# Layer 0 of a two-layer perceiver kernel: from rows of whole tiles to one list of half tiles on the same three rotating PSUM banks

## The chip, the cores and the metric

One core of one Trainium2 chip. The metric is the device time of the whole kernel in microseconds (us). Engines: PE (TensorE, matmuls, with PEld for its weight loads), DVE (VectorE), ACT (ScalarE), POOL (GpSimd), SP (SyncE, issues the DMAs).

## The reference, cut to what matters

A block of two layers over a latent x [128, 256] and a context of 12544 rows of 192. The change touches the first cross attention alone:

```python
def _L0_xattn_ref(query, key_value, Wq, bq, Wk, bk, Wv, bv, Wo, bo):   # 16 heads of 16
    q = (query @ Wq + bq).reshape(B, Nq, H, D).transpose(0, 2, 1, 3)
    k = (key_value @ Wk + bk).reshape(B, Nkv, H, D).transpose(0, 2, 1, 3)
    v = (key_value @ Wv + bv).reshape(B, Nkv, H, D).transpose(0, 2, 1, 3)
    attn = jnp.einsum('bhqd,bhkd->bhqk', q, k) * scale
    attn = jnp.clip(attn, -CLAMP, CLAMP)
    attn = jax.nn.softmax(attn, axis=-1)
    x = jnp.einsum('bhqk,bhkd->bqhd', attn, v).reshape(B, Nq, Cq)
    return x @ Wo + bo
```

Behind it come a gated attention, a feed-forward with ternary weights, and the same three for layer 1.

## The kernel before

**Tiling of layer 0.** The 12544 context rows are worked in 14 chunks (NCH) of 896 columns (CH), each of 7 tiles (TPC) of 128 keys, each tile in two halves (HALVES = 14 per chunk) of 8 heads. All 128 queries and 16 heads are done at once, with a running maximum per head, so a chunk needs its maxima before its scores. A round of the loop therefore scores and weighs chunk c and prepares chunk c + 1. The letters of the work, as the kernel's list names it:
- K (4 per chunk, `project0`): a key block, 5 matmuls of 448 columns; ACT writes its high part (`key_block_hi`), DVE its low part (`key_block_lo`). SP then stacks the keys by 12 DMAs (`stack_keys`).
- m (32, `unit_scores`): one matmul over 32 rows that gives a head's (and its pair's) scores of half a chunk; DVE takes the maximum (`unit_max`, L918). Four neighbours lie in four row groups. Behind m 18 and m 31 DVE merges the maxima (`half_maxima`, L926 to L936).
- V (7, `values0`): a tile of values, 5 matmuls of 256; ACT copies it (`value_tile`).
- R (4, `minus_max_row`): minus the maxima as rows, cast by ACT into the queries' extra row (`max_row`). The diagonal that R multiplies is made by POOL for the first half (`spread_half`, L469) and by DVE for the second.
- L: whether any maximum is so large that clipping is needed (`large_sum`, `clip_flag`). With these inputs it is not, and `clip_half` is branched over.
- F (`factors`): how far the maximum fell, transposed; ACT copies it, DVE rescales the running sum in bank 4 (`rescale`, L995).
- S (14 halves, `scores0`): 4 matmuls of 256 into banks 0 and 1 or 2 and 3; ACT takes the exponential of 1024 columns (`exponentials`, L668).
- W (14 halves, `weigh0`): 8 float32 products (16 records) of 17 weight columns, added up in bank 4.

ACT also casts the raw context of chunk c + 2 to its high part (`split_hi0`, L607 and L609), POOL then makes the low parts (`split_lo0`, L457 and L460), and SP loads the next raw chunk.

**What sets the order.** Every engine has its own in-order queue, written out from one list, `LIST`: one row for each of the 7 tiles. K, F, m, V, R and L take the three PSUM banks 5 to 7 in turn; `bank_free` makes PE wait for whoever reads the bank's last use. An S in a row is a whole tile (both halves), a W too:

```python
LIST = [["K0", "F", "K1", "S", "K2", "K3", "W", "m", "m", "m", "V0", "V1", "m", "m", "V2", "V3", "m", "m"]]
LIST += [["S", "m", "m", "m", "W", "m", "m"]] * 5
LIST += [["W", "R0", "R1", "V4", "V5", "V6", "R2", "R3", "L", "", "", "S"]]
```

ACT casts both parts of the raw chunk together, behind the first row. POOL's loop makes the spread of chunk c + 1 and then the low parts of chunk c + 2. In the last round nothing is prepared; there PE adds two sums for the feed-forward's ternary thresholds behind the second tile (L1497, L1499), after DVE's two sums over the weights (L1026). From them POOL makes the ternary weights (L508 to L512), while layer 0 ends and the gated attention runs.

Of the kernel before, what the change touches and what calls it, by code (L numbers as in the profile page):

```python
# [22 lines left out]
ALU = mybir.AluOpType  # L23
ACT = mybir.ActivationFunctionType
# [60 lines left out]
def steps():  # L85

    out, n, m = [], 0, 0
    for items in LIST:
        row = []
        for item in items:  # L90
            if item in ("S", "W"):
                row.append((item, 0, None))
                continue
            kind, i = item[:1], int(item[1:] or 0)
            if kind == "m":
                i, m = m, m + 1
            if kind:
                row.append((kind, i, n))
            n += 1
        out.append(row)  # L100
    return out, n


STEPS, USES = steps()
BANKS = 3
USED_BY = {n: (kind, i) for row in STEPS for kind, i, n in row if n is not None}
assert USES % BANKS == 0


def use_bank(n):  # L110
    return 5 + n % BANKS


def bank_of(kind, i):
    return use_bank(next(n for n, use in USED_BY.items() if use == (kind, i)))


def user_before(n):

    at = n - BANKS  # L120
    while at % USES not in USED_BY:
        at -= BANKS
    kind, i = USED_BY[at % USES]
    return kind, i, at < 0
# [29 lines left out]
def perceiver(nc, a, out):  # L154
    with ExitStack() as ctx:
# [273 lines left out]
        def _(pool):  # L429
# [49 lines left out]

            pool.wait_ge(S["qs_rows"], 192)  # L480
            spread_half(0, 0)
            pool.wait_ge(S["e0_dm_half"], 1)
            split_lo0(1, 1)
            pool.wait_ge(S["e0_lo"], 3)
# [95 lines left out]
        def _(act):  # L580
# [21 lines left out]
            def split_hi0(c, b, half=None):  # L602

                if half != 1:
                    act.wait_ge(S["e0_raw"], 48 * (c + 1))
                    act.wait_ge(S["e0_vproj"], TPC * (c - 1))
                    nc.scalar.copy(ct[:, b, X_AH, :], raw[:, 0, :])  # L607
                if half != 0:
                    nc.scalar.copy(ct[:, b, X_B, :], raw[:, 1, :]).then_inc(S["e0_hi"], 1)  # L609
# [32 lines left out]
            act.wait_ge(S["e0_raw"], 48)  # L642
            nc.scalar.copy(ct[:, 0, X_AH, :], raw[:, 0, :])
            nc.scalar.copy(ct[:, 0, X_B, :], raw[:, 1, :]).then_inc(S["e0_hi"], 1)
            for i in range(4):
                key_block_hi(0, i)
            act.wait_ge(S["v_ones"], 2)
            for t in range(4):
                value_tile(0, 0, t)
            act.wait_ge(S["e0_raw"], 96)  # L650
            nc.scalar.copy(ct[:, 1, X_AH, :], raw[:, 0, :])
            nc.scalar.copy(ct[:, 1, X_B, :], raw[:, 1, :]).then_inc(S["e0_hi"], 1)
            for i in range(2):
                max_row(0, i)
            for t in range(4, TPC):
                value_tile(0, 0, t)
            for i in range(2, 4):
                max_row(0, i)
            fall_spread(0)

            def exponentials(c, b, t):

                for u in (2 * t, 2 * t + 1):
                    g = HALVES * c + u
                    act.wait_ge(S["e0_ok"], g + 1)
                    act.wait_ge(S["e0_score"], g + 29)
                    act.wait_ge(S["e0_pv"], g + 11)
                    nc.scalar.activation(pr[:, (HALVES * b + u) % 4, :], bank(2 * (u % 2), 2), ACT.Exp  # L668
                                         ).then_inc(S["e0_exp"], 1)

            exponentials(0, 0, 0)

            def chunk0(c, b, i2, nxt=True, split=True):

                for t in range(TPC):
                    for kind, i, n in STEPS[t]:
                        if kind == "S" and t < TPC - 1:
                            exponentials(c, b, t + 1)
                        elif kind == "F":
                            factor_copy(c)  # L680
                        elif not nxt:
                            continue
                        elif kind == "S":
                            fall_spread(c + 1)
                            exponentials(c + 1, 1 - b, 0)
                        elif kind == "K":
                            if i == 0:
                                act.wait_ge(S[f"e0_keys{b}"], 192 * (i2 + 1))
                                act.wait_ge(S["e0_head"], UNITS * (c + 1))
                            key_block_hi(c + 1, i)  # L690
                        elif kind == "V":
                            if i == 0:
                                act.wait_ge(S["e0_pv"], HALVES * (c + 1))
                            value_tile(c + 1, 1 - b, i)
                        elif kind == "R":
                            if i % 2 == 0:
                                act.wait_ge(S["e0_score"], HALVES * (c + 1) + 27 + i // 2)
                                act.wait_ge(S["e0_row_out"], 16 * (c + 1))
                            max_row(c + 1, i)
                    if split and t == 0:  # L700
                        split_hi0(c + 2, b)

# [3 lines left out]
            chunk0(NCH - 2, 0, NSUP - 1, split=False)  # L706
            chunk0(NCH - 1, 1, NSUP - 1, nxt=False, split=False)
# [115 lines left out]
        def _(dve):  # L823
# [88 lines left out]
            def unit_max(c, m, n):  # L912

                h, half = unit_of(m)[4], unit_of(m)[3]
                if m % 16 == 0:
                    dve.wait_ge(S["e0_chain"], 8 * c)
                dve.wait_ge(S["e0_head"], UNITS * c + m + 1)
                V.tensor_reduce(cu2[:, h, half:half + 1], ps[:, use_bank(n), 0:NB], AX_X, ALU.max  # L918
                                ).then_inc(S["e0_red"], 1)
# [44 lines left out]
            def prepare(c, b, t, flag):  # L964

                for kind, i, n in STEPS[t]:
                    if kind == "S" and (t < TPC - 1 or c < NCH):
                        clip(c - 1 + (t + 1) // TPC, (t + 1) % TPC, flag)
                    elif c == NCH:
                        if kind == "K" and i == 1:  # L970
                            rescale(c - 1)
                    elif kind == "K":
                        key_block_lo(c, i)
                        if i == 1 and c > 0:
                            rescale(c - 1)
                    elif kind == "m":
                        unit_max(c, i, n)
                        if i == 18:
                            half_maxima(c, b, 0)
                        if i == UNITS - 1:  # L980
                            half_maxima(c, b, 1)
                            after_maxima(c, b)
                    elif kind == "L":
                        flag = clip_flag(c)
                        with dve.If(flag < 1):
                            dve.sem_inc(S["e0_ok"], HALVES)
                            dve.sem_inc(S["clip_min"], HALVES)
                            dve.sem_inc(S["clip_max"], HALVES)
                return flag

# [21 lines left out]
            def clip(c, t, flag):  # L1012

                if flag is not None:
                    with dve.If(flag > 0):
                        clip_half(c, 2 * t)
                        clip_half(c, 2 * t + 1)

            flag = None
            for c in range(-1, NCH):  # L1020
                for t in range(TPC):
                    flag = prepare(c + 1, (c + 1) % 2, t, flag)
                    if c == NCH - 1 and t == 0:
# [270 lines left out]
        def _(pe):  # L1294
# [37 lines left out]
            def bank_free(c, n):  # L1332

                kind, i, earlier = user_before(n)
                x = c - 1 if earlier else c
                if kind == "K":
                    pe.wait_ge(S["e0_klo"], 4 * x + i + 1)
                elif kind == "F":
                    pe.wait_ge(S["e0_factor_sb"], c)
# [6 lines left out]
                elif kind == "L":  # L1346
                    pe.wait_ge(S["e0_clipf"], x + 1)
# [458 lines left out]
```

## Time and profile before

| | |
|---|---|
| median of 3 runs | 920.91 us (920.09 to 921.3) |
| the profiled execution | 919.66 us, span 917.8 us |
| granted TensorE clock, mean | 0.97 |
| PE busy | 857.3 us (93%) |
| DVE busy | 628.9 us (69%) |
| ACT busy | 427.2 us (47%) |
| POOL busy | 217.6 us (24%) |

The span runs from the first to the last instruction of the profiled execution. Busy times are unions of an engine's instructions; matmuls overlap each other, so the distance between their starts tells more than their durations. The second tenth of the span to its middle (some 60 to 515 us) is the rounds of layer 0.

### The profile page before, as it was taken

The page shows a single profiled execution, that of the slowest core. Times are in us where ns is not written, and L with a number is a line of the kernel's source. Part 1 is how long each engine was busy: PE and PEld are TensorE (multiplying, and loading weights), DVE is VectorE, ACT ScalarE, POOL GpSimd, SP SyncE. Part 2 cuts the span into 40 slices and gives each one's busy share as a digit, 9 for nine tenths or more (in the row PEclk, how much of TensorE's full clock was granted, in tenths as well). Part 3 has the DMA queues.
Part 4 walks back from the last instruction along what each step waited for, and adds up shares of the span by engine and source line. Part 5 has one row for each costly group of instructions (what it writes and reads, how often), then busy time and mean ns, then how long its engine had stood idle before and what let it go on. Part 6 is the DMA issues. An engine that isn't in the chain of part 4 may idle for free.

```text
span 917.8 us, 21933 instructions
## 1 busy us (share of the span) xinstructions
PE 857.3 (93%) x7662; PEld 663.3 (72%) x7662; DVE 628.9 (69%) x1104; ACT 427.2 (47%) x578; POOL 217.6 (24%) x233
## 2 busy tenths in 40 slices
PE   3889999999999999999999988998999999999798
PEld 2567777777777777777777757654688887888676
DVE  5768568568568568567567643699487878777373
ACT  2245765765765766766765721300233333333122
POOL 4182022022022022022020392350033232222000
PEclk9669999999999999999999999999999999999798
DMA  5845645645645645648635133210000000000000
GB/s 178 197 128 124 180 114 120 178 115 120 175 118 120 172 120 120 170 123 211 168 85 122 48 139 106 81 39 1 7 19 13 18 14 19 13 19 7 1 1 7
DMA packets 43867, 85.16 MB, mean 93 GB/s; under 512 B 11616, under 2 KB 26657, under 8 KB 41889
## 3 DMA queue, kind: packets, MB, share of 16 engines
q1 hardware_dynamic: 43822, 84.62, 35.9%
q8 instruction: 21, 0.34, 0.2%
q14 instruction: 24, 0.19, 0.1%
HBM read 45.03 MB, written 0.25 MB: 49 GB/s over the span
## 4 chain that ended last, share of the span: by engine, by line
PE 69%; issue 12%; DVE 10%; POOL 4%; ACT 2%; SPq 1%; DMA 1%; DVEq 0%; ACTq 0%; POOLq 0%
PE ps L1642 9%; PE ps L1455 9%; PE ps L1467 8%; PE ps L1373 8%; PE ps L1363 7%; PE ps L1356 6%; DVE cu L918 6%; PE ps L1650 5%; PE ps L1663 5%; PE ps L1643 2%; PE ps L1382 1%; PE ps L1389 1%; POOL ffw L510 1%; POOL wraw L508 1%; PE ps L1616 1%
## 5 line engine op out<-in xcount | busy, mean ns | idle before, releaser
L918 DVE TENSOR_REDUCE cu<-ps 128x1 f32<-128x448 f32 x448 | 250.4, 618 | 53.2 <-PE ps L1373 51.2
L668 ACT ACTIVATE pr<-ps 128x1024 f32<-128x1024 f32 x196 | 190.1, 1023 | 66.4 <-PE ps L1455 65.6
L435 POOL TENSOR_TENSOR pause<-pause 128x1 f32<-128x1 f32 x41 | 12.8, 314 | 569.5 <-DVE mr L930 377.5
L1373 PE MATMUL ps<-khl,qp 32*128 32x448 f32 x448 | 123.9, 483 | 2.6 <-DVE khl L908 0.8
L1455 PE MATMUL ps<-qs,ks 128*128 128x256 f32 x784 | 122.6, 296 | 3.3 <-ACT qs L627 3.1
L1455 PEld LDWEIGHTS ps<-qs,ks 128*128 128x128 f32 x784 | 101.9, 190 | 21.7 <-issue 20.6
L1467 PE MATMUL ps<-pr,v 128*17 128x128 f32 x3136 | 104.6, 274 | 0.5 <-DVE ps L995 0.5
L1642 PE MATMUL ps<-ks,ct 128*128 128x512 f32 x352 | 98.2, 400 | 0.3 <-ACT pr L788 0.3
L1467 PEld LDWEIGHTS ps<-pr,v 128*17 128x17 f32 x3136 | 77.2, 97 | 22.2 <-issue 19.1
L1373 PEld LDWEIGHTS ps<-khl,qp 32*128 32x128 f32 x448 | 57.9, 188 | 48.9 <-DVE cu L918 14.0
L908 DVE SCALAR_TENSOR_TENSOR khl<-ps,bk,khl 128x448 fp32r<-128x448 f32 x56 | 37.1, 682 | 74.5 <-ACT khl L615 74.5
L1206 DVE TENSOR_SCALAR ps<-ps 128x1024 f32<-128x1024 f32 x44 | 54.1, 1229 | 46.2 <-PE ps L1643 46.2
L788 ACT ACTIVATE pr<-ps 128x1024 f32<-128x1024 f32 x44 | 45.3, 1030 | 81.3 <-DVE ps L1206 81.3
L1642 PEld LDWEIGHTS ps<-ks,ct 128*128 128x128 f32 x352 | 64.8, 189 | 17.6 <-issue 3.4
L1363 PE MATMUL ps<-wv,ct 128*128 128x256 f32 x490 | 72.9, 298 | 4.5 <-DVE cu L918 3.6
L1363 PEld LDWEIGHTS ps<-wv,ct 128*128 128x128 f32 x490 | 65.3, 194 | 15.3 <-DVE cu L918 7.9
L1356 PE MATMUL ps<-ct,wk 128*128 128x448 f32 x280 | 68.9, 387 | 2.1 <-DVE khl L908 2.1
L621 ACT COPY v<-ps 128x256 f32<-128x256 f32 x98 | 36.6, 374 | 60.3 <-PE ps L1363 59.1
L1189 DVE TENSOR_TENSOR pr<-pr,wraw 128x1024 f32<-128x1024 f32 x45 | 55.0, 1223 | 4.0 <-issue 4.0
L1356 PEld LDWEIGHTS ps<-ct,wk 128*128 128x128 f32 x280 | 52.5, 198 | 6.4 <-DVE khl L908 2.5
L1193 DVE TENSOR_TENSOR nm<-nm,pr 128x1024 f32<-128x1024 f32 x45 | 55.4, 1232 | 1.5
L1173 DVE CUSTOM_DVE_ANT_0 pr<-ps,khl 128x1024 f32<-128x1024 f32 x48 | 55.5, 1220 | 0.0
(263 smaller groups left out, 1143.7 us busy)
## 6 DMA issues: line engine op xcount, KB each, us to landing
ks<-khl SPq DMA_DIRECT2D x168, 224.0 KB, 4.9
nm<-maxima SPq DMA_DIRECT2D x14, 1024.0 KB, 4.6
raw<-in_ctxT SPq DMA_DIRECT2D x14, 448.0 KB, 3.9
raw<-in_ctxT SPq DMA_DIRECT2D x28, 224.0 KB, 4.4
ffw<-in_mask_q SPq DMA_DIRECT2D x1, 1568.0 KB, 9.6
raw<-in_ctxT SPq DMA_DIRECT2D x12, 128.0 KB, 2.2
raw<-in_ctxT SPq DMA_DIRECT2D x22, 64.0 KB, 1.8
raw<-in_ctxT SPq DMA_DIRECT2D x44, 32.0 KB, 2.0
```

What stands on the lines that cost most here:

```text
L668: nc.scalar.activation(pr[:, (HALVES * b + u) % 4, :], bank(2 * (u % 2), 2), ACT.Exp).then_inc(S["e0_exp"], 1)
L918: V.tensor_reduce(cu2[:, h, half:half + 1], ps[:, use_bank(n), 0:NB], AX_X, ALU.max).then_inc(S["e0_red"], 1)
L1173: nc.vector.tensor_tensor_reduce(out=junk[:, h % 2], in0=ps[:, 2 * (h % 4):2 * (h % 4) + 2, :], in1=negm[:, b, :].bitcast(F32).rearrange(" ...
L1189: V.tensor_tensor(sl, sl, mk[:, u // 2, :].unsqueeze(1).to_broadcast([P, 8, T]), ALU.mult).then_inc(S["e1_masked"], 1)
L1193: V.tensor_tensor(acc, acc, pr[:, u, :], ALU.add).then_inc(S["e1_sum"], 1)
L1206: V.tensor_scalar(bank(2 * (u % 2), 2), bank(2 * (u % 2), 2), 80.0, None, ALU.min).then_inc(S["e1_ok"], 1)
L1356: last = mm(dst, wk0[:, w, t * P:(t + 1) * P], ct[:, b, xx, half * NB:(half + 1) * NB], start=(j == 0), stop=(j == 4))
L1363: last = mm(ps[:, use_bank(n), 0:C], ct[:, b, xx, t * P:(t + 1) * P], wv0[:, w, :], start=(j == 0), stop=(j == 4))
L1373: mm(ps[:, use_bank(n), 0:NB], qp[part, t, e, :], khl[part, 0, t, half * NB:(half + 1) * NB], start=True, stop=True).then_inc(S["e0_head"], 1)
L1455: last = mm(ps[:, 2 * z + k // 2, (k % 2) * 256:(k % 2) * 256 + 256], ks_v[:, b, gg, t * P:(t + 1) * P], qs[:, gg * 256:gg * 256 + 256], s ...
L1467: last = mm(ps[32 * j:32 * j + 17, 4, (h // 4) * T:(h // 4 + 1) * T], v17_v[:, b, t, h, :], pr[:, (HALVES * b + u) % 4, k * T:(k + 1) * T] ...
L1642: mm(ps[:, 2 * z + j, :], cu[:, t, xx, :], asp[:, w, cols], start=(i == 0), stop=False)
```

## The change

The list becomes one sequence of words, cyclic over rounds, with S and W as single halves; every other word means what it did (X is DVE's rescale, H one of ACT's two casts of the raw chunk, E ACT's exponential of the fall of the maxima, _ a bank left out). The K of the next chunk still stand in front, now with V0 ahead of them and V1 behind. The head and the tail of layer 0 are the same list with what has no chunk left out, instead of code of their own. Banks 0 to 3 are booked by the same table as banks 5 to 7. On POOL the low parts of chunk c + 2 come before the spread of chunk c + 1. ACT's two casts stand apart. The two sums for the thresholds stand behind W7 of the last round, DVE's sums over the weights behind S3.

```diff
-LIST = [["K0", "F", "K1", "S", "K2", "K3", "W", "m", "m", "m", "V0", "V1", "m", "m", "V2", "V3", "m", "m"]]
-LIST += [["S", "m", "m", "m", "W", "m", "m"]] * 5
-LIST += [["W", "R0", "R1", "V4", "V5", "V6", "R2", "R3", "L", "", "", "S"]]
+ORDER = (
+    "V K K F S X K K V W m m m S V H m m S m m W W m m m S S W m m m W S V m m W W _ m m H m S W m m "
+    "S S m m W S m m S m V m m m R W R m m W m m V S V _ W W R R L W E S S "
+).split()
...
             with pool.Fori(2, NCH, 2) as c:
                 for b in range(2):
+                    split_lo0(c + b, b)
+                    pool.wait_ge(S["e0_lo"], c + b + 2)
                     spread_half(c + b - 1, 1 - b)
-                    split_lo0(c + b, b)
...
+                    elif kind == "H":
+                        split_hi0(x, xb, i)
+                    elif kind == "K":
+                        if i % 2 == 0 and (not isinstance(c, int) or x > 0):
+                            act.wait_ge(S[f"e0_keys{1 - xb}"], 192 * (x2 + xb))
+                            act.wait_ge(S["e0_head"], UNITS * (x - 1) + 8 * i + 16)
+                        key_block_hi(x, i)
...
+                    if isinstance(c, int) and c == NCH - 1 and (kind, i) == ("W", 7):
+                        pe.wait_ge(S["e0_red"], UNITS * NCH)
...
-                if t == 1:
-                    pe.wait_ge(S["e0_red"], UNITS * NCH)
```

PE's queue in the middle of a round (S is L1455, m L1373, W L1467; REGISTER_ALU are PE's waits with a computed count). Before:

```order
L1455 MATMUL ps<-qs,ks 128x256 x4
L1452 REGISTER_ALU
L1455 MATMUL ps<-qs,ks 128x256 x4
L1343 REGISTER_ALU
L1373 MATMUL ps<-khl,qp 128x448
L1341 REGISTER_ALU
L1373 MATMUL ps<-khl,qp 128x448
L1341 REGISTER_ALU
L1373 MATMUL ps<-khl,qp 128x448
L1463 REGISTER_ALU
L1467 MATMUL ps<-pr,v 17x128 x16
```

After (S is L1402, m L1373, V L1363), behind the first three m of a round:

```order
L1402 MATMUL ps<-qs,ks 128x256 x4
L1339 ISA
L1363 MATMUL ps<-wv,ct 128x256 x5
L1339 REGISTER_ALU
L1373 MATMUL ps<-khl,qp 128x448
L1339 REGISTER_ALU
L1373 MATMUL ps<-khl,qp 128x448
L1332 REGISTER_ALU
L1402 MATMUL ps<-qs,ks 128x256 x4
L1341 REGISTER_ALU
L1373 MATMUL ps<-khl,qp 128x448
```

Where a whole tile of S stood between m and W, a half tile now stands with a V, or alone.

POOL's queue in the loop, one round: the spread is L469, the low parts are L457 and L460. Before:

```order
L466 ISA
L467 REGISTER_ALU [waits e0_chain]
L435 TENSOR_TENSOR pause<-pause 128x1 [waits e0_row]
L469 TENSOR_TENSOR dm<-con,mr 128x1024
L455 REGISTER_ALU
L457 TENSOR_TENSOR ct<-raw,ct 128x896 [waits e0_lo,e0_hi]
L460 TENSOR_TENSOR ct<-raw,ct 64x896 [waits e0_alo]
```

After, the low parts are L479 and L482, the spread is L491:

```order
L479 TENSOR_TENSOR ct<-raw,ct 128x896 [waits e0_lo,e0_hi]
L482 TENSOR_TENSOR ct<-raw,ct 64x896 [waits e0_alo]
L520 REGISTER_ALU
L488 ISA [waits e0_lo]
L489 REGISTER_ALU [waits e0_chain]
L457 TENSOR_TENSOR pause<-pause 128x1 [waits e0_row]
L491 TENSOR_TENSOR dm<-con,mr 128x1024
```

The low parts no longer wait behind the maxima (e0_chain), and the spread waits behind both.

PE's queue in the last round, up to the two sums (F is L1389, the sums are L1497 and L1499). Before:

```order
L1389 MATMUL ps<-con,wraw 128x128 x4
L1455 MATMUL ps<-qs,ks 128x256 x8
L1467 MATMUL ps<-pr,v 17x128 x16
L1455 MATMUL ps<-qs,ks 128x256 x8
L1467 MATMUL ps<-pr,v 17x128 x16
L1497 MATMUL ps<-con,cnt 49x1
L1499 MATMUL ps<-wsum,con 128x2
```

After (the sums are L1461 and L1463):

```order
L1402 MATMUL ps<-qs,ks 128x256 x4
L1414 MATMUL ps<-pr,v 17x128 x8
L1402 MATMUL ps<-qs,ks 128x256 x8
L1414 MATMUL ps<-pr,v 17x128 x16
L1402 MATMUL ps<-qs,ks 128x256 x8
L1414 MATMUL ps<-pr,v 17x128 x16
L1402 MATMUL ps<-qs,ks 128x256 x4
L1414 MATMUL ps<-pr,v 17x128 x16
L1402 MATMUL ps<-qs,ks 128x256 x4
L1414 MATMUL ps<-pr,v 17x128 x8
L1461 MATMUL ps<-con,cnt 49x1
L1463 MATMUL ps<-wsum,con 128x2
```

Eight halves of W now stand ahead of the sums, where four stood.

## Rows read from the trace of the kernel before

**Rows 1.** The page: span, and busy time of each engine with its share.

```profile
span 917.8 us, 21933 instructions
PE 857.3 (93%) x7662; PEld 663.3 (72%) x7662; DVE 628.9 (69%) x1104; ACT 427.2 (47%) x578; POOL 217.6 (24%) x233
```

**Rows 2.** One line's instructions: the rescale; count, durations in ns, first and last start.

```profile
L995 DVE TENSOR_TENSOR ps<-ps,wraw x14: 689/690/699, 66.6 to 513.5; 128x512 f32<-128x512 f32 x14
```

**Rows 3.** Ten rounds: length, busy us by engine, granted clock, DMA share, GB/s.

```profile
132.30:477.68 345.38, 338.69 (x3811) 263.57 (x3810) 236.59 (x480) 232.00 (x331) 62.03 (x40) 1.00 0.56 141
```

**Rows 4.** The timeline of PE, one round: start, us, what, idle before it.

```profile
198.79 0.73 PE L1455 MATMUL ps<-qs,ks 128*128 128x256 f32 x4
199.74 0.73 PE L1455 MATMUL ps<-qs,ks 128*128 128x256 f32 x4 [0.21 <-ACT qs L627]
...
203.36 1.12 PE L1455 MATMUL ps<-qs,ks 128*128 128x256 f32 x8
204.31 2.19 PE L1356 MATMUL ps<-ct,wk 128*128 128x448 f32 x10
206.43 1.07 PE L1467 MATMUL ps<-pr,v 128*17 128x128 f32 x32
207.43 0.98 PE L1373 MATMUL ps<-khl,qp 32*128 32x448 f32 x3
208.68 1.46 PE L1363 MATMUL ps<-wv,ct 128*128 128x256 f32 x10 [0.27 <-DVE cu L918]
...
215.14 0.62 PE L1373 MATMUL ps<-khl,qp 32*128 32x448 f32 x2
215.69 1.22 PE L1455 MATMUL ps<-qs,ks 128*128 128x256 f32 x8
216.84 0.51 PE L1373 MATMUL ps<-khl,qp 32*128 32x448 f32 x3
217.28 1.07 PE L1467 MATMUL ps<-pr,v 128*17 128x128 f32 x32
```

**Rows 5.** The timeline of DVE and POOL around the first half's maxima.

```profile
221.67 0.16 DVE L926 TENSOR_TENSOR cm<-cu 128x8 f32<-128x8 f32 x1
...
222.14 3.40 DVE L918 TENSOR_REDUCE cu<-ps 128x1 f32<-128x448 f32 x6
...
224.40 2.10 POOL L457 TENSOR_TENSOR ct<-raw,ct 128x896 fp32r<-128x896 f32 x1
...
226.58 2.10 POOL L460 TENSOR_TENSOR ct<-raw,ct 64x896 fp32r<-64x896 f32 x1
```

**Rows 6.** L926 over the kernel, and the timeline of DVE and POOL before the first round.

```profile
L926 DVE TENSOR_TENSOR cm<-cu x28: 156/162/3283, 43.4 to 506.4; 128x8 f32<-128x8 f32 x28
...
50.88 3.28 DVE L926 TENSOR_TENSOR cm<-cu 128x8 f32<-128x8 f32 x1
...
50.60 3.53 POOL L489 TENSOR_TENSOR ffw<-ffw 128x1568 int32<-128x1568 int32 x1
```

**Rows 7.** The timeline of the last round, around the two sums.

```profile
514.12 4.47 DVE L1026 TENSOR_REDUCE wsum<-ffw 128x1 f32<-128x2048 f32 x2
514.26 0.79 PEld L1467 LDWEIGHTS ps<-pr,v 128*17 128x17 f32 x32 [0.67 <-DVE ps L995]
...
515.26 1.22 PE L1455 MATMUL ps<-qs,ks 128*128 128x256 f32 x8
...
516.41 1.07 PE L1467 MATMUL ps<-pr,v 128*17 128x128 f32 x32
...
518.64 0.38 PE L1499 MATMUL ps<-wsum,con 128*128 128x2 f32 x2 [0.98 <-DVE wsum L1026]
...
520.06 2.92 POOL L508 TENSOR_SCALAR wraw<-ffw,thr 128x1024 f32<-128x1024 f32 x1 [19.43 <-issue]
```

**Rows 8.** The chain of work that ended last, where it leaves POOL: start, us, what.

```profile
553.77 0.57 POOL rstd L443
554.37 0.42 DVE xn L856
```

More of the change, by code:

```diff
@@ new lines, with order @@
+EARLY_KEYS, EARLY_UNITS = 0, 0
+UNITS = 2 * H
+def order():
+    out, seen, uses = [], dict.fromkeys("SWKVRmHFXEL", 0), 0
+    for word in ORDER:
+        kind = "m" if word[0] == "u" else word[0]
+        ring = 5 + uses % 3
+        uses += word[0] in "mKVRFL_"
+        if kind == "_":
+            continue
+        n = seen[kind]
+        seen[kind] = n + 1
+        if kind == "S":
+            later, i = divmod(n + 2, HALVES)
+            banks = (2 * (i % 2), 2 * (i % 2) + 1)
+        elif kind == "W":
+            later, i, banks = 0, n, ()
+        elif kind == "K":
+            later, i = divmod(n + EARLY_KEYS, 4)
+            later, banks = later + 1, (ring,)
+        elif kind == "m":
+            later, i = divmod(n + EARLY_UNITS, UNITS)
+            later, banks = later + 1, (int(word[1]),) if word[0] == "u" else (ring,)
+        elif kind in "FX":
+            later, i, banks = int(seen["W"] > 0), 0, (ring,) if kind == "F" else ()
+        elif kind == "H":
+            later, i, banks = 2, n, ()
+        else:
+            later, i, banks = 1, n, () if kind == "E" else (ring,)
+        out.append((kind, i, banks, later))
+    assert uses % 3 == 0
+    return out
@@ new lines, with done_in, user_before @@
+STEPS = order()
+USERS = {b: [at for at, step in enumerate(STEPS) if b in step[2]] for b in (0, 1, 2, 3, 5, 6, 7)}
+def done_in(c):
+    return [(at, kind, i, banks, later) for at, (kind, i, banks, later) in enumerate(STEPS)
+            if not isinstance(c, int) or 0 <= c + later < NCH]
+def user_before(c, at, b):
+    users, back = USERS[b], 0
+    k = users.index(at)
+    while not isinstance(c, int) or c - back >= -2:
+        k -= 1
+        if k < 0:
+            k, back = len(users) - 1, back + 1
+        kind, i, _, later = STEPS[users[k]]
+        if not isinstance(c, int) or 0 <= c - back + later < NCH:
+            return kind, i, later - back
+    return None
@@ L127, in unit_of @@
+def bank_of(kind, i):
+    return next(banks[0] for k, n, banks, _ in STEPS if (k, n) == (kind, i))
 def unit_of(m):
@@ L651, in _ @@
[L651 to L701, printed above, removed]
@@ L1407, in weigh_tile @@
-            def weigh_tile(c, b, t):
-                if t == 0:
-                    pe.wait_ge(S["e0_scaled"], c + 1)
-                for z in range(2):
-                    weigh0(c, b, 2 * t + z)
-            def step0(c, b, count, t, first=False, only=None):
-                x, xb = c + 1, 1 - b
-                for kind, i, n in STEPS[t]:
-                    if kind == "S" and not first:
-                        if t < TPC - 1:
-                            tile(c, b, count, t + 1)
-                        elif only is None:
-                            tile(c + 1, 1 - b, count + b, 0)
-                    elif kind == "W" and not first:
-                        weigh_tile(c, b, t)
-                    elif kind not in "SW":
-                        prepare(x, xb, kind, i, n, first, only)
@@ L1428, in prepare @@
[L1428 to L1448 removed]
+                mm(ps[:, n, 0:1], ones, large[:, :], start=True, stop=True).then_inc(S["e0_flag"], 1)
```

284 lines of the change are left out of this document (137 added, 147 removed).

## The prediction

> **What bounds the kernel now.** I read the page first [rows 1]: TensorE (PE) is busy for 93% of a span of 917.8 us, VectorE (DVE) 69%. The change touches layer 0 alone, which is 14 rounds, one per chunk of keys. The line that rescales the running sum once per round starts first at 66.6 and last at 513.5 us [rows 2]: 13 rounds in 446.9 us, 34.4 us each. Inside them [rows 3] PE is busy for 338.69 of 345.38 us at a granted clock of 1.00, DVE for 236.59, ACT for 232.00. So a round is PE's own queue, and only what PE's queue costs or waits for counts.
>
> What PE's 34.4 us consist of is read in the order of its runs [rows 4]. I call K, V, S, R, F, L full forms (128 rows, 128 columns of weights), m the head maxima (32 rows of weights) and W the weighing (17 columns). Starts, not durations, are the measure, since matmuls overlap:
> - Eight matmuls of S between two K take 204.31 - 203.36 = 0.95 us. Eight between two m runs take 216.84 - 215.69 = 1.15. **A stretch of full forms that has m or W on both sides costs 0.20 more.**
> - A run of three m, in three different row groups, takes 217.28 - 216.84 = 0.44. One of two takes 215.69 - 215.14 = 0.55, longer, because the second waited for a bank. So an m run costs 0.44 however short it is, if its banks are free.
> - W for a whole tile takes 207.43 - 206.43 = 1.00.
> - Waits: m x3 and what follows up to V take 208.68 - 207.43 = 1.25 instead of 0.44 (0.8 lost to the low key halves and a bank); the second S half at a round's start comes 199.74 - 198.79 = 0.95 behind the first, where four matmuls after an m or L need some 0.58 (0.4 lost to the cast of the last maxima row).
>
> **The change, in one round.** The same matmuls are issued; what changes is how often PE changes form. Counted in the two lists (cyclically, with F at the start):
> - Stretches of full forms: 8 before, 14 after. 6 x 0.20 = +1.2 us.
> - Stretches of W: 7 before (a whole tile each), 11 after (eight of them half tiles alone). No half alone is in the trace. Between 0 (a half is just half of 1.00) and 0.2 (the price of both ends of a full stretch); I take 0.1, one end. 4 x 0.1 = +0.4.
> - m runs: 13 before, 14 after. +0.4.
> Together **+2.0 us per round**, certain in sign as long as PE is the bound.
>
> Against it stand the waits that go. S0 and S1 of the next chunk now come behind L and a W half, so the cast of the last maxima row has 0.55 us more: -0.4. V no longer stands directly behind the first three m, only the low key halves are waited for: -0.4. In the five regular rounds of S m m m W m m a second or third m waits some 0.1 to 0.25 each (0.55 against 0.44 above); in the new order the m groups are spread as unevenly (2, 2, 3, 3, 2, 3, 2, 2, 2, 2, 1, 3, 2, 2) and three banks are still all there are, while a reduction takes 3.40 / 6 = 0.57 us [rows 5]; I give half of these back, -0.4, and -0.2 for what stood at V and R late in the round. Bounds: nothing (DVE paces m as before) to -3 (every wait goes). I take **-1.4**.
>
> Then the cost that the change brings on POOL. Before, POOL makes the spread (L469) and after it the two low halves of the chunk after next (L457, L460: 224.40 to 228.68) [rows 5], and the three small DVE instructions of the first half of the maxima (from L926, 221.67) come while POOL is idle: 0.16 us for the first. Now POOL does the low halves first, as soon as ACT has cast the second half. ACT's second cast stands behind V3, ahead of m 17; the maxima stand behind m 18. A cast, a signal and two times 2.1 us of POOL cover the next 4 to 5 us, and m 18's reduction is some 3 us behind the cast. So L926 should fall into the second of POOL's instructions. What happens then is in the trace once [rows 6]: L926 began at 50.88 beside POOL's L489 (50.60 to 54.13) and took 3.28 us, until POOL's instruction ended. The reductions from PSUM are not held this way: the six of L918 from 222.14 to 225.54, at 0.57 each, run on beside L457. DVE stands up to 2.1 us, 1.6 by the positions; PE has three banks and some S and W to do in the meantime, which cover about a third: **+1.0** per round, bounds 0 and 2.1. The Trainium skill (GPSIMD Engine Reference, the table of the engine's properties) says that GpSimd shares its SBUF interfaces with VectorE and contends with DVE instructions in a two-port mode or with two SBUF inputs; L926 is one with two SBUF inputs, and the 3.28 us agree.
>
> Sum of a round: 2.0 - 1.4 + 1.0 = +1.6 us, 13 rounds: **+20.8**. I shade it to +1.4 and **+18**, since the list of waits is the softest term and can only be larger than I found.
>
> **The last round.** Its end is not what counts. The thresholds of the FFN weights are made from L1499's sums, and from them POOL works without a pause from 520.06 [rows 7] to 554.34, where the chain of work goes on at DVE's L856 [rows 8]. L1499 stands behind the second W tile and waits for L1026 (514.12 to 518.59): 518.64. Now it stands behind W7. From W0 (514.26, one start before the S x8 at 515.26) PE has S3 S4, W1 W2, S5 S6, W3 W4, S7, W5 W6, S8, W7. S x8 between W takes 516.41 - 515.26 = 1.15, a W tile 1.00, half tiles 0.67 and 0.55: 0.55 + 1.15 + 1.0 + 1.15 + 1.0 + 0.67 + 1.0 + 0.67 + 0.5 = 7.7. So the sums come at about 522.0 on the old scale, with L1026 long done, against 518.64: **+3.3** (bounds +2, if S and W halves cost nothing extra, and +5, if the exponentials hold W7). The tiles behind W7 are hidden under POOL's 34 us as before.
>
> **The start.** The first V is projected while DVE is still held, but ACT copies it ahead of the first two key blocks, which costs about 1 us; in return the V blocks no longer come two at a time between the m there. POOL's low halves ahead of the spread can hold L926 here too. I take **0**, bounds -3 and +3.
>
> Sum: 18 + 3.3 + 0 = +21. The profiled execution took 919.66 us (span 917.8 and 1.9 around it), 1.2 below the median of 920.91; 919.66 + 21 = 941, and on the scale of the median **942 us**.
>
> **Rivals.**
> 1. *No collision with POOL.* If ACT's second cast runs late (V3 late) or early, POOL's instructions miss L926. Then +0.6 per round, 13 x 0.6 + 3.3 = +11: 932. For it: in the old trace L926 took 162 ns in the median of 28 [rows 6]. Against: the places in the lists. Chance 0.22.
> 2. *The waits were the larger part, and the new order is faster.* Where 3 of the about 3.4 us of waits per round go and the changes of form come at half price, the round has 1.0 - 3.0 = -2.0 at best; with a third of a us of collision about -0.8, 13 times: -10, + 3: 914. It decides once more than 2.2 us of waits go in a round. For it: PE's busy share of 98% hides waits, as the 1.25 for three m shows. Against: the 0.20 of the row of S. The Trainium skill (TensorE: Matmul & The Clock Gate, Part 2) says that LDWEIGHTS is pulled ahead of running matmuls when row groups don't conflict or the background buffer is the target; by that rule changes of form between such tiles would be free. The rows of S do not bear it out. Chance 0.17.
> 3. *Nothing to see.* Changes and waits cancel and the collision is small: 919 to 923. Chance 0.06.
> The forecast, forms plus collision, has 0.55.
>
> **How the numbers follow.** Forecast alone: 934 to 953 (+0.9 to +2.2 per round, the last with the collision at full price). With rival 1 below and part of rival 2 the range is 917 to 953. A difference under 0.2% (1.8 us) can't be told from no change. Faster: 0.17; within: 0.05; slower: 0.78.
>
> **What the profile would show.** Right: the rescale line's starts 35.5 to 36 us apart; S x4 between m or W at 0.67 or so; L926's mean far over 0.2 us, beside POOL's low halves; POOL's thresholds starting 3 us later behind the last rescale. Wrong: rounds under 34.4 us, which would mean that my waits were counted too low; L926 at 0.16, which takes out 1.0 per round; or a new wait at R for POOL's spread, which now comes behind 4.2 us of other work and would add to the time.

## The result, and the profile after

The changed kernel takes **982.33 us** in the median of 4 runs (980.82 to 984.26), the kernel before 920.58 beside it (920.09 to 921.3): a ratio of 1.067 [1.066, 1.069] (in brackets, here and below, the 95% interval). The direction is the one predicted. The size is three times it, 62 us where 21 were forecast.

The page of the changed kernel, span and busy times, and the row of the granted clock in 40 slices (they answer to [rows 1]):

```profile
span 981.3 us, 22063 instructions
PE 913.7 (93%) x7662; PEld 683.6 (70%) x7662; DVE 653.5 (67%) x1104; ACT 430.5 (44%) x578; POOL 217.4 (22%) x233
PEclk9669979889898897897997998999999999999898
```

PE has the same 7662 matmuls and is busy for 56 us more. The same work took longer, and the clock's row is full of sevens and eights. The rescale line (it answers to [rows 2]), and the stretch from its first to its last start in both kernels, the windows view with its columns as in [rows 3]:

```profile
L971 DVE TENSOR_TENSOR ps<-ps,wraw x14: 699/700/700, 71.7 to 576.1; 128x512 f32<-128x512 f32 x14
71.70:576.10 504.40, 494.51 (x4938) 361.48 (x4936) 330.04 (x623) 302.27 (x425) 76.90 (x50) 0.90 0.49 121
```

```profile
66.60:513.50 446.90, 437.86 (x4941) 340.22 (x4940) 306.53 (x624) 298.42 (x426) 76.49 (x50) 1.00 0.55 137
```

The span grew by 63.5 us. The first rescale comes 5.1 us later, the 13 rounds take 504.4 instead of 446.9 (**57.5 more**), and what lies behind the last rescale grew from 404.3 to 405.2 (0.9). In the rounds the mean granted clock went from 1.00 to 0.90. PE's idle time in them hardly changed, 446.90 - 437.86 = 9.0 us before and 504.40 - 494.51 = 9.9 after. How one round looks, from 211.3 to 300.0 (2.3 rounds):

```profile
211.30:221.50 10.20, 10.02 (x72) 6.36 (x75) 6.00 (x14) 3.26 (x6) 0.00 (x0) 0.50 0.06 18
221.50:252.20 30.70, 30.13 (x321) 22.64 (x313) 20.11 (x35) 20.65 (x28) 6.24 (x4) 1.00 0.62 154
252.20:259.00 6.80, 6.56 (x46) 3.95 (x47) 3.93 (x10) 1.49 (x3) 0.00 (x0) 0.50 0.00 0
259.00:289.80 30.80, 30.33 (x336) 23.38 (x334) 21.13 (x39) 21.58 (x30) 6.24 (x4) 1.00 0.59 147
289.80:300.00 10.20, 10.02 (x72) 6.36 (x75) 6.00 (x14) 3.27 (x7) 0.00 (x0) 0.50 0.07 20
```

**Once per round TensorE runs at 1.2 GHz** (0.50) instead of 2.4, for 6.8 and 10.2 us in turn, 12 times between the first and the last rescale; in the kernel before the clock between the two is 1.00. What stands ahead of the fall at 252.20: DVE, POOL and PE from 243 (timeline as in [rows 4]).

```profile
245.78 1.63 DVE L929 TENSOR_TENSOR cm<-cu 128x8 f32<-128x8 f32 x1
...
247.72 3.40 DVE L921 TENSOR_REDUCE cu<-ps 128x1 f32<-128x448 f32 x6
...
243.10 2.10 POOL L479 TENSOR_TENSOR ct<-raw,ct 128x896 fp32r<-128x896 f32 x1 [33.00 <-ACT ct L633]
245.28 2.10 POOL L482 TENSOR_TENSOR ct<-raw,ct 64x896 fp32r<-64x896 f32 x1
...
246.28 0.47 PE L1373 MATMUL ps<-khl,qp 32*128 32x448 f32 x2
246.68 0.63 PE L1414 MATMUL ps<-pr,v 128*17 128x128 f32 x16
247.24 0.73 PE L1402 MATMUL ps<-qs,ks 128*128 128x256 f32 x4
248.40 1.00 PE L1373 MATMUL ps<-khl,qp 32*128 32x448 f32 x2 [0.42 <-DVE cu L921]
249.32 0.74 PE L1402 MATMUL ps<-qs,ks 128*128 128x256 f32 x4
249.99 0.47 PE L1373 MATMUL ps<-khl,qp 32*128 32x448 f32 x1
...
252.44 0.79 PE L1382 MATMUL ps<-dm,nsel 128*128 128x512 f32 x1 [0.26 <-DVE cu L921]
253.16 1.06 PE L1414 MATMUL ps<-pr,v 128*17 128x128 f32 x16
```

The collision is where the prediction put it. L929 (L926 of before) begins at 245.78, in POOL's second low half (245.28 to 247.38), and ends with it: 1.63 us instead of the 0.16 of [rows 5]. The next six reductions come late, PE waits 0.42 us for a bank up to 248.40, and 3.8 us behind that the clock falls. S x4 at 247.24 and the m run at 248.40 hold PE for 1.16 and 0.92 us, where the S x4 at 249.32 and the m run at 246.28 hold it 0.67 and 0.40: 1.0 us for the collision. The W half at 253.16 then holds PE until 254.14, 0.98 us; at 246.68 it was 0.56.

### The profile page after: what moved, and what is told of

Read it like the earlier page. It is cut to its first block, busy times and chain, and to the rows that moved or that the text cites. A ratio compares the mean times of both kernels' runs of the same rounds, so it can differ in the third digit from the quotient of the medians.

```text
span 981.3 us, 22063 instructions
## 1 busy us (share of the span) xinstructions
PE 913.7 (93%) x7662; PEld 683.6 (70%) x7662; DVE 653.5 (67%) x1104; ACT 430.5 (44%) x578; POOL 217.4 (22%) x233
## 4 chain that ended last, share of the span: by engine, by line
PE 71%; issue 13%; DVE 10%; POOL 3%; SPq 1%; ACT 1%; DMA 1%; DVEq 0%; POOLq 0%; ACTq 0%
PE ps L1373 10%; PE ps L1414 10%; PE ps L1402 9%; PE ps L1614 9%; PE ps L1363 7%; PE ps L1354 6%; PE ps L1622 5%; PE ps L1635 4%; DVE cu L921 4%; PE ps L1382 3%; PE ps L1615 2%; DVE cm L929 2%; PE ps L1389 1%; POOL wraw L531 1%; POOL ffw L533 1%
## 5 line engine op out<-in xcount | busy, mean ns | idle before, releaser
L672 ACT ACTIVATE pr<-ps 128x1024 f32<-128x1024 f32 x196 | 196.2, 1024 | 105.7 <-PE ps L1402 100.9
L1373 PE MATMUL ps<-khl,qp 32*128 32x448 f32 x448 | 138.6, 518 | 9.5 <-DVE cu L921 7.6
L1402 PE MATMUL ps<-qs,ks 128*128 128x256 f32 x784 | 137.5, 308 | 0.3 <-ACT pr L672 0.2
L1414 PE MATMUL ps<-pr,v 128*17 128x128 f32 x3136 | 127.4, 295 | 1.6 <-DVE ps L971 1.4
L1402 PEld LDWEIGHTS ps<-qs,ks 128*128 128x128 f32 x784 | 108.3, 199 | 26.9 <-issue 20.6
L479 POOL TENSOR_TENSOR ct<-raw,ct 128x896 fp32r<-128x896 f32 x14 | 29.5, 2110 | 405.4 <-ACT ct L633 378.8
L1373 PEld LDWEIGHTS ps<-khl,qp 32*128 32x128 f32 x448 | 60.2, 201 | 67.5 <-DVE cu L921 26.1
L1363 PE MATMUL ps<-wv,ct 128*128 128x256 f32 x490 | 90.8, 324 | 0.1
L1363 PEld LDWEIGHTS ps<-wv,ct 128*128 128x128 f32 x490 | 77.6, 222 | 9.9 <-DVE cu L921 6.4
L791 ACT ACTIVATE pr<-ps 128x1024 f32<-128x1024 f32 x44 | 45.3, 1029 | 81.3 <-DVE ps L1195 81.3
L1354 PE MATMUL ps<-ct,wk 128*128 128x448 f32 x280 | 63.9, 376 | 2.8 <-DVE khl L911 2.8
L457 POOL TENSOR_TENSOR pause<-pause 128x1 f32<-128x1 f32 x41 | 13.5, 331 | 235.1 <-DMA raw<-in_ctxT 161.4
L651 ACT CAST qs<-ps 32x512 fp32r<-32x512 f32 x56 | 31.0, 577 | 58.4 <-PE ps L1382 58.4
## 6 DMA issues: line engine op xcount, KB each, us to landing
ffw<-in_mask_q SPq DMA_DIRECT2D x1, 1568.0 KB, 10.2
```

The lines of the kernel that those rows point to most:

```text
L791: nc.scalar.activation(pr[:, u, :], bank(2 * (u % 2), 2), ACT.Exp).then_inc(S["e1_exp"], 1)
L1354: last = mm(dst, wk0[:, w, t * P:(t + 1) * P], ct[:, b, xx, half * NB:(half + 1) * NB], start=(j == 0), stop=(j == 4))
L1363: last = mm(ps[:, n, 0:C], ct[:, b, xx, t * P:(t + 1) * P], wv0[:, w, :], start=(j == 0), stop=(j == 4))
L1373: mm(ps[:, n, 0:NB], qp[part, t, e, :], khl[part, 0, t, half * NB:(half + 1) * NB], start=True, stop=True).then_inc(S["e0_head"], 1)
L1402: last = mm(ps[:, 2 * z + k // 2, (k % 2) * 256:(k % 2) * 256 + 256], ks_v[:, b, gg, t * P:(t + 1) * P], qs[:, gg * 256:gg * 256 + 256], s ...
L1414: last = mm(ps[32 * j:32 * j + 17, 4, (h // 4) * T:(h // 4 + 1) * T], v17_v[:, b, t, h, :], pr[:, (HALVES * b + u) % 4, k * T:(k + 1) * T] ...
```

## The experiments

All ran beside the kernel before, which took 918.06 to 918.39 us beside e1 to e9; times are medians, ratios are to those. A difference under 2% is called neither faster nor slower here: e3 and e6 to e9 count as the same as before, and e2 is at that border. Their table, with the stretch from the first to the last rescale of one profiled execution each:

| kernel | us | ratio | first rescale | 13 rounds | clock there |
|---|---|---|---|---|---|
| before | 920.58 | | 66.6 | 446.9 | 1.00 |
| after | 982.33 | 1.067 [1.066, 1.069] | 71.7 | 504.4 | 0.90 |
| e1: POOL's loop order undone | 942.51 | 1.026 [1.020, 1.031] | 73.3 | 459.7 | 0.99 |
| e2: ahead of the loop as well | 936.09 | 1.018 [1.014, 1.022] | 68.0 | 464.3 | 0.98 |
| e3: before, POOL's order alone | 918.01 | 1.001 [0.997, 1.004] | 67.6 | 446.9 | 1.00 |
| e4: after, with eight more matmuls | 958.39 | 1.042 [1.037, 1.046] | 73.9 | 476.1 | 1.00 |
| e5: before, with the collision | 962.97 | 1.049 [1.045, 1.053] | 68.0 | 487.9 | 0.95 |
| e6: after's code, old list | 915.76 | 0.997 [0.994, 1.000] | 62.6 | 445.6 | 1.00 |
| e6b: e6 with POOL's old order | 922.04 | 1.004 [1.002, 1.007] | 68.1 | 445.6 | 1.00 |
| e7: a list of my own | 920.29 | 1.003 [1.000, 1.006] | 65.9 | 443.7 | 1.00 |
| e8: a second one | 918.72 | 1.001 [0.998, 1.004] | 72.8 | 440.1 | 1.00 |
| e9: e8 with POOL's new start | 911.51 | 0.994 [0.991, 0.997] | 61.5 | 440.1 | 1.00 |

The 13 rounds are the firm part: e3 and the kernel before have 446.9 both, e6 and e6b 445.6, e8 and e9 440.1. The start and the end are not. The changed kernel, e1 and e4 have the same code up to the first rescale and reach it at 71.7, 73.3 and 73.9 us; e3 has the same code as before behind the last rescale and takes 401.9 us there instead of 404.3. So a difference of 2 us in the start or the end of single profiles tells nothing.

### The list without the collision: e1 and e2

e1 takes POOL's order in the loop back to that of before, and leaves the list:

```
-                    split_lo0(c + b, b)
-                    pool.wait_ge(S["e0_lo"], c + b + 2)
                     spread_half(c + b - 1, 1 - b)
+                    split_lo0(c + b, b)
```

e2 does the same ahead of the loop, where the split of chunk 1 goes back behind the spread.

> The changed kernel with one thing undone: in the loop POOL makes the spread of the maxima before the low parts, as before the change. Theory A (the blocked maxima and the clock that falls behind them): L929 is back at 0.17 us, the stall of PE behind m 21 goes, the granted clock stays at 1.00 in the rounds, a round is 35.0 to 35.6 us instead of 39.3, in all 930 to 940. Rival (the changes of form and short runs themselves make PE too sparse, the clock falls anyway): L929 at 0.17, but the clock still falls once a round, 38 us a round, 965 to 972.

> As the run with POOL's loop order undone, and the same order undone ahead of the loop too (the spread of chunk 0 before the low parts of chunk 1). The first rescale came at 71.7 us after the change and 66.6 before. Theory: POOL's order is the cause there too (L933 stood 6.1 us once), so this run has the first rescale at 66 to 68 and is 4 us under the other. Rival: the V ahead of the keys and the copy of V0 ahead of the key blocks are: the first rescale stays at 70 to 72 and the two runs are equal.

The maxima's line is back at 0.16 us in the rounds, and 40 and 46 us are gone. e1's rounds are as its first theory has them, its time 2.5 us above 940. All rounds but the last and those with a fall take 35.2 to 35.5 us, against 34.5 to 34.7 before. e2's last three have a fall of 6.8 us each, and one of e1's; such a round takes 37.6 to 37.8 (the last of e2 35.6, where the changed kernel's last takes 33.2). The stretch of e2 around one fall:

```profile
434.00:444.00 10.00, 9.67 (x105) 6.46 (x103) 8.07 (x17) 6.85 (x9) 4.99 (x4) 0.99 1.00 295
443.90:450.70 6.80, 6.80 (x48) 4.18 (x49) 3.89 (x10) 1.53 (x3) 1.29 (x1) 0.50 0.49 138
```

and around e1's:

```profile
111.00:131.00 20.00, 19.90 (x229) 13.69 (x227) 15.76 (x30) 13.12 (x17) 4.62 (x4) 1.00 0.67 140
131.00:138.00 7.00, 6.85 (x48) 4.23 (x49) 4.21 (x11) 1.53 (x3) 1.57 (x1) 0.52 0.46 133
```

So two prices: **the list alone costs 0.8 us per round at full clock, a fall of 6.8 us costs 2.3 to 2.4.** This list runs close to a fall even without the collision. **The falls of e1 and e2 need no wait of PE**: ahead of e1's PE is busy for 19.90 of 20 us. They begin beside the first R of the round, where the 6.8-us falls of the changed kernel begin too. What tips the list in three rounds and not in ten isn't seen in these rows.

### POOL's order in the old list: e3 and e5

e3 gives the kernel before POOL's new order in the loop and puts ACT's second cast behind t = 1; e5 puts it behind t = 2. e5's edit:

```
-                    spread_half(c + b - 1, 1 - b)
                     split_lo0(c + b, b)
+                    pool.wait_ge(S["e0_lo"], c + b + 2)
+                    spread_half(c + b - 1, 1 - b)
...
-                    if split and t == 0:
-                        split_hi0(c + 2, b)
+                    if split and t in (0, 2):
+                        split_hi0(c + 2, b, t // 2)
```

> The kernel before, its list untouched, with the collision alone: POOL makes the low parts ahead of the spread in the loop, and ACT's second cast stands one tile later, so that POOL's second low part covers L926. Theory A: L926 at 1.0 to 2.1 us in the rounds, PE stalls behind m 21; if the stall alone brings the clock down, 3 to 5 us a round, 960 to 985. Rival (the clock needs the sparse order of half tiles as well): 0.8 to 1.5 us a round, clock at 1.00, 930 to 940.

> The earlier attempt to bring the collision into the old list missed: POOL was done 1.3 us before L926, which stayed at 0.16 us. Here ACT's second cast stands one more tile later (behind the third), so POOL's second low part should lie over the first half's maxima. List untouched. Theory A (a stall of PE behind blocked maxima brings the clock down by itself): L926 (here L927) at 1 to 2 us, clock at half for 6 to 10 us in each round, 37 to 39 us a round, 950 to 980. Rival (it takes the sparse order of half tiles too): 35.2 to 36 us a round, clock at 1.00, 927 to 940.

e3 missed its aim: POOL's second instruction ended at 221.35, the maxima began at 222.62 and took 0.16 us. It shows only that POOL's order by itself costs nothing in the old list. e5 hit, with 2.03 us for the maxima in 12 rounds, and is 45 us slower than before with the old list and the same matmuls. DVE, POOL and PE of one round:

```profile
236.66 2.03 DVE L927 TENSOR_TENSOR cm<-cu 128x8 f32<-128x8 f32 x1
...
236.57 2.10 POOL L460 TENSOR_TENSOR ct<-raw,ct 64x896 fp32r<-64x896 f32 x1
...
237.19 1.22 PE L1456 MATMUL ps<-qs,ks 128*128 128x256 f32 x8
239.68 1.52 PE L1374 MATMUL ps<-khl,qp 32*128 32x448 f32 x3 [1.27 <-DVE cu L919]
...
242.56 2.08 PE L1456 MATMUL ps<-qs,ks 128*128 128x256 f32 x8
244.56 0.74 PE L1374 MATMUL ps<-khl,qp 32*128 32x448 f32 x3
```

and its clock in the windows view:

```profile
239.00:242.40 3.40, 2.59 (x37) 1.52 (x37) 3.28 (x7) 0.99 (x2) 2.04 (x2) 1.00 0.73 213
242.40:245.80 3.40, 3.40 (x25) 2.55 (x27) 1.62 (x3) 1.91 (x2) 0.00 (x0) 0.51 0.20 57
```

PE waits 1.27 us for a bank, the clock falls 2.7 us behind that, and S x8 at 242.56 holds PE for 2.00 us where it holds it 1.15 at full clock [rows 4]. The chain is the same as in the changed kernel, so the changed list isn't needed for it; the wait is three times as long here, though. Nine rounds take 37.6 us with 3.4 us at half clock, three 39.1 with 6.8: the time per round is in the range of theory A, the half clock is shorter than its 6 to 10 us. Of the 3.1 us that a round of 37.6 is longer than before 1.27 is the wait; by subtraction 1.8 is left for the clock.

### The stall with the wait filled: e4

e4 keeps everything of the changed kernel, POOL's order and the collision too, and computes two S halves twice, just ahead of and behind the place where PE waits. It does more work than the reference wants:

```
-                for k in range(4):
+                for k in list(range(4)) * (1 + twice):
...
-                        scores0(x, xb, i)
+                        scores0(x, xb, i, twice=i in (11, 12))
```

> The changed kernel with S11 and S12 of each round computed twice (eight more matmuls of 256 columns, the same values into the same banks), which puts PE work where it waits behind the blocked maxima. Theory A (the clock falls because PE is sparse there): the clock stays up in most rounds, 36.5 to 37 us a round although more is computed, 945 to 955. Rival (the clock falls for another reason, or the fill is too small): 39.3 to 40 a round, 982 to 992.

**With eight more matmuls per round the kernel is 24 us faster.** DVE's stall is there, the wait behind it isn't, and neither is the fall:

```profile
238.07 1.65 DVE L929 TENSOR_TENSOR cm<-cu 128x8 f32<-128x8 f32 x1
...
239.53 1.21 PE L1402 MATMUL ps<-qs,ks 128*128 128x256 f32 x8
240.71 1.00 PE L1373 MATMUL ps<-khl,qp 32*128 32x448 f32 x2
241.64 1.21 PE L1402 MATMUL ps<-qs,ks 128*128 128x256 f32 x8
242.78 0.46 PE L1373 MATMUL ps<-khl,qp 32*128 32x448 f32 x1
```

```profile
73.90:550.00 476.10, 468.79 (x5042) 352.06 (x5040) 329.13 (x624) 302.12 (x425) 77.00 (x50) 1.00 0.52 128
```

Between the starts of the S stretch and of the next m run lie 1.18 us here and 1.16 in the changed kernel (247.24 to 248.40), where four matmuls and a wait of 0.42 fill them: half of the added work cost nothing. The theory that the collision costs its own wait and no more falls with this run: by it more work can't make a round shorter, and the rounds take 36.8 us instead of 39.3 (the time, 958, is 3 us above what was expected). The second half of the added work costs 242.78 - 241.64 = 1.14 us instead of 0.67, 0.5 more. Without it e4's round would take 36.35 us at full clock, 1.0 above e2's 35.35: the price of the collision a second time. The run doesn't tell whether the matmuls help because they stand in the wait or only because they are more work in the round.

### The rest of the change: e6 and e6b

e6 is the changed kernel with the words of the old list, e6b puts POOL's order back as well:

```
-    "V K K F S X K K V W m m m S V H m m S m m W W m m m S S W m m m W S V m m W W _ m m H m S W m m "
-    "S S m m W S m m S m V m m m R W R m m W m m V S V _ W W R R L W E S S "
+    "K F K X S S K K W W m m m V V m m V V m m H H S S m m m W W m m S S m m m W W m m S S m m m W W m m "
+    "S S m m m W W m m S S m m m W W m m W W R R V V V R R L _ _ E S S "
```

> The changed kernel's code with the old list written in its words (whole tiles, V behind the first m, both casts together), with POOL's new order and the sums behind W7. If the list is what costs: 34.5 us a round, clock at 1.00; first rescale near 67; the last round's sums 3 us later; in all 918 to 926. Rival (the code around the list costs too, more waits with computed counts, half tiles booked one by one): 35 us or more a round, 930 and up.

> The code of the changed kernel with the list of the kernel before, and with POOL's three places (ahead of the loop, and in it) put back to those of before. Against the run with POOL's new places (first rescale at 62.6 us, 34.4/34.5 us per round, 915.8 us) it shows what POOL's new place ahead of the loop is worth where the list is the old one. Theory A (POOL's place ahead of the loop gives the earlier start): the first rescale comes at 66 to 67 us as in the kernel before, rounds 34.4/34.5, the time 918 to 920. Theory B (the earlier start comes from the rest of the code, the other places of the first blocks' copies): first rescale near 62.6 again and 915 to 917 us. No fall of the granted clock inside layer 0's rounds by either.

Rounds are 34.4 and 34.5 us in both, as before, so nothing around the list costs anything in them, and with the old list the same code has no fall. The first rescale stands at 62.6 in e6, where 67 was expected, and at 68.1 in e6b: POOL's new order ahead of the loop is worth 5.5 us there, by the first theory of e6b's expectation (POOL's loop begins at 72.1 in e6, too late to matter for it).

### Lists of my own: e7, e8, e9

They use the same words in another order, with POOL's loop order of before. e8's list, the better one, keeps full forms together more often than the changed list does (12 stretches of them instead of 14, four W halves alone instead of eight):

```
+    "F K K X K K S S m m W W m H m V V V m m S m m S V m H m W W m m S m m S W m m m S W m m W S m m m W "
+    "S m m S m m W W m m S S m m W W m m R W W R V V V R R L E S _ S _ "
```

e9 is e8 with POOL's low halves ahead of the spread before the loop only.

> A list of my own in the changed kernel's code, POOL's order as before: whole tiles as in the old list, but a single S or W at four places so that three m find three free banks, the rescale ahead of the other key blocks, S ahead of the first m, and V ahead of more m. By the prices of the trace (0.20 for a stretch of full forms, 0.44 for an m run, waits for banks) a round comes to 0.7 us under the old one: 33.8 us, 908 to 916 in all if the clock stays. Rival (the waits come back elsewhere, or the clock falls): 920 or more.

> A second list by the same prices, with more single halves early in the round (fewer waits, more changes of form): 0.6 us under the old round by the prices, 34.0 us, 910 to 918. Rival: the changes of form cost more than priced, or PE gets sparse and the clock falls: 925 or more.

> The same list as the second list of my own (rounds of 34.0 us, but a first rescale at 72.8 us), with POOL's old order in the loop and its new order ahead of the loop. Theory A (POOL's place ahead of the loop sets the start): the first rescale comes about 4 us earlier, 68 to 69 us, rounds 34.0, so 914 to 916 us, which would be below both kernels. Theory B (the list itself makes the start late, since its first blocks stand in another order): the first rescale stays at 72 to 73 us and the time at 918 to 919.

e7 has rounds of 34.2 and e8 of 34.0 us, 0.3 and 0.5 below before. e8's rounds are as forecast, e7's 0.4 us longer than forecast, and neither time is in its range. e7's 3 us are gone behind the last rescale (408.6 us to the end of the span instead of 404.3), most of e8's 7 at the start (72.8 instead of 66.6) and 2 behind; of that some 2 us at either end may be the spread named above. **e9 is the fastest of all, 911.51 us, 0.6% below the kernel before by the ratio, and the only one whose whole interval lies below 1.** Its rounds are e8's. Its first rescale comes 11.3 us earlier, where theory A had about 4. e8's start, its maxima beside POOL's unpacking of the FFN weights:

```profile
57.57 3.28 DVE L928 TENSOR_TENSOR cm<-cu 128x8 f32<-128x8 f32 x1
...
61.08 1.68 DVE L932 TENSOR_SCALAR mr<-mx 128x8 fp32r<-128x8 f32 x1
...
57.30 8.70 POOL L511 TENSOR_TENSOR ffw<-ffw 128x1568 int32<-128x1568 int32 x5
```

and e9's:

```profile
51.18 0.84 DVE L928 TENSOR_TENSOR cm<-cu 128x8 f32<-128x8 f32 x1
...
52.26 0.88 DVE L932 TENSOR_SCALAR mr<-mx 128x8 fp32r<-128x8 f32 x1
...
46.59 8.69 POOL L511 TENSOR_TENSOR ffw<-ffw 128x1568 int32<-128x1568 int32 x5
```

The clock there, e8 and then e9, from 60 to 75 us:

```profile
60.00:75.00 15.00, 11.99 (x64) 10.54 (x67) 8.32 (x14) 8.34 (x13) 11.77 (x6) 0.69 0.28 102
```

```profile
60.00:75.00 15.00, 15.00 (x156) 11.54 (x155) 11.49 (x20) 10.90 (x15) 1.43 (x1) 1.00 0.84 202
```

With the changed list the same swap of POOL's work goes the other way: the first rescale comes 5.3 us later (e1 against e2). How much of either difference is stall, how much clock and how much POOL's own order isn't separated.

## Why the prediction was right or wrong

**What failed is the first step**: "Inside them [rows 3] PE is busy for 338.69 of 345.38 us at a granted clock of 1.00", and from it that only what PE's queue costs or waits for counts. Every later term was priced at that clock, and none asks what the new order or a wait of PE does to the clock. The 57.5 us of the rounds by the runs:

| term | predicted per round | measured |
|---|---|---|
| the list, forms less waits | +2.0 - 1.4 = +0.6 | +0.8 (e2: 35.35 against 34.55) |
| the collision | +1.0 | about +1.0 |
| the clock | not in the sum | about +3.0 |

The last row: a round of the changed kernel with 6.8 us at half clock takes 38.7, one with 10.2 takes 39.9. The first kind has 2.35 of it from the fall (e1, e2), the second 1.2 more, so 2.95 in the mean and 35 us over 12 rounds. 38.7 - 2.35 - 35.35 gives 1.0 for the collision, 12 us in all. The list makes 0.8 x 12 and 0.8 in the last round, 10 us. Together 57. At full clock the round would have cost 1.8 us more, where the sum had 1.6 and the text shaded to 1.4: **the terms that the sum had came out near their sizes, and a term of more than one and a half times their sum was missing**. The split hangs together: the price of a fall comes from e1 and e2, the 1.0 of the collision from e4 too, and from the rows around 248 us.

That the stall is what brings a fall into every round is shown: without it the list had one fall and three in 13 rounds (e1, e2), with it 12. The stall alone isn't the whole cause. The list has a part in it, since falls come in it without any stall and never in the old list without one (before, e3, e6, e6b). e5 shows that a longer wait is enough in the old list, e4 that more work takes the falls away with the stall still there.

The trace of before had a warning, behind the rounds. The windows from 540 to 562 us, where PE stands beside POOL's thresholds:

```profile
540.00:555.00 15.00, 9.76 (x75) 7.13 (x75) 5.15 (x13) 3.96 (x8) 13.99 (x7) 1.00 0.01 2
555.00:562.00 7.00, 7.00 (x44) 6.58 (x45) 2.03 (x4) 2.26 (x3) 0.00 (x0) 0.76 0.00 0
```

PE is busy for 9.76 of 15 us at full clock, and fully busy behind it at 0.76. That is a far larger gap than the one of a round, and how small a gap is enough no row of before tells; but it shows that this clock falls within the kernel, behind a stretch in which PE has less to do, and it could have made a rival above 953 us. The Trainium skill (TensorE: Matmul & The Clock Gate, Part 1) says that a gate sets the clock by how busy PE has been lately, and tells of a kernel whose short pauses between groups of matmuls bring it down over and over. The 12 falls here agree, and so does e4, in which more work takes them away; the busy time of the trace doesn't tell the rounds apart, since e1's fall stands behind 19.90 busy us of 20. By the penalty that the Trainium skill gives in the same part, half of the time at half clock, the mean of 8.5 us per round would cost an estimated 4.25 us; by the rows a fall costs 3.0.

**By single steps:**
- *A change of form.* S x8 between W takes 578.59 - 577.45 = 1.14 us in the changed kernel's last round (rows below) and an S half 0.67, as predicted. A W half takes 0.56 where half of a whole tile's 1.00 is 0.50: eight of them make +0.5 where 0.4 stood. e2's +0.8 for the whole list leaves 1.2 to 1.3 for the waits that went (1.4 predicted); this is a remainder, the waits were not measured one by one. The prediction's row of m groups is short of one m (the list has 3, 2, 2, 3, 3, 2, 3, 2, 2, 2, 1, 3, 2, 2); its count of 14 is right, and nothing hangs on the row.
- *The place of the collision.* ACT's second cast at 242.07, POOL's instructions at 243.10 and 245.28, the maxima at 245.78: in the second one, as predicted, and 1.63 us long ("1.6 by the positions").
- *Rivals.* The first, no collision, was e1 and e2 in effect: forecast 932 at 0.6 a round, measured 942 and 936 at 0.8, with a few falls and the start in them. The second, a faster list, doesn't hold for this list but does in the rounds of others (e7, e8, e9). The third, nothing to see, doesn't hold. 982 lies 29 us above the end of the range; no rival had a time above 932. A wait at R for POOL's spread didn't arise.
- *The last round.* The sums stand behind W7 now:

```profile
576.89 0.63 PE L1414 MATMUL ps<-pr,v 128*17 128x128 f32 x16 [1.39 <-DVE ps L971]
577.45 1.21 PE L1402 MATMUL ps<-qs,ks 128*128 128x256 f32 x8
578.59 1.07 PE L1414 MATMUL ps<-pr,v 128*17 128x128 f32 x32
...
581.93 0.74 PE L1402 MATMUL ps<-qs,ks 128*128 128x256 f32 x4
582.60 1.07 PE L1414 MATMUL ps<-pr,v 128*17 128x128 f32 x32
...
585.01 0.38 PE L1463 MATMUL ps<-wsum,con 128*128 128x2 f32 x2
...
586.42 2.92 POOL L531 TENSOR_SCALAR wraw<-ffw,thr 128x1024 f32<-128x1024 f32 x1 [24.09 <-issue]
```

  From W0 to the sums 585.01 - 576.89 = 8.1 us (7.7 predicted), and POOL begins 10.3 us behind the last rescale where it was 6.6 [rows 7]: +3.7 for the predicted +3.3. From the last rescale to the end it is only +0.9, though. Behind POOL's start the changed kernel takes 394.9 us and the one before 397.7; these 3 us are little more than the spread of that stretch, and the end's clock falls lie at other places in the two.
- *The start.* 0 was predicted, within 3; it is +5.1, of which some 2 can be spread. e2, with POOL's old order, has +1.4. The maxima of chunk 0's second half come 5 us later than before and run into POOL's MEMSET:

```profile
56.25 6.10 DVE L933 TENSOR_SCALAR mr<-mx 128x8 fp32r<-128x8 f32 x1
...
56.25 6.07 POOL L515 MEMSET ks<- 32x7168 f32 x1
```

  The price of a collision is what is left of POOL's instruction, and POOL's longest ones stand here. The bounds took their lengths from the low halves alone (2.1 us).

## What to carry to other kernels

Where TensorE is busy for 98% of a round at full clock, a new wait can have two prices: its own, and that of the slower clock that may follow; here a stall of 1.6 us on another engine cost 1 us as a wait and 3 us as a clock, in every round but the last. Read the granted clock behind every place of the old trace where TensorE waits, try matmuls of the same round where the wait will be, and compare the whole order by its clock before its count of form changes. A new order can come close to a fall without any wait, as e1 and e2 show. When work moves on GpSimd, check in the old trace which small VectorE instructions with operands in SBUF have lasted until a GpSimd instruction ended, and where those fall in the new order.

## What the runs showed of the hardware

- A wait of 0.42 us in PE's work stood ahead of 6.8 to 10.2 us at 1.2 GHz in 12 of 13 rounds of the changed kernel; with the same stall and eight more matmuls per round there was none. More work made the kernel 24 us faster. What decides between a fall and none was not found: e2's list had three falls in 13 rounds with the same instructions in each but the last, and e1's one fall stood behind 20 us with PE busy for 19.90.
- At 1.2 GHz not everything takes twice as long: the W half took 0.98 instead of 0.56 us, S x8 2.00 instead of 1.15, and 6.8 us of it cost a round 2.3 to 2.4 us.
- A VectorE instruction of 8 columns took 0.84, 1.63, 2.03, 3.28 or 6.10 us, each time until the GpSimd instruction beside it ended, also one with a single tensor operand in SBUF (L933, beside a MEMSET that reads none). VectorE's reductions from PSUM went on at 0.57 each. Not every small one is held: a TENSOR_SCALAR of one column with its operand in SBUF (L1042 of before, at 521.23) took 0.16 us inside POOL's L508 (520.06 to 522.98).
